# A recurrent mixer scheduled in double slots of two head pairs, its gated output kept in SBUF, and feed-forward first sums kept apart by parity

## The chip, the cores and the metric

The kernel runs on one core of one Trainium2 chip. The metric is the device time of one execution in microseconds (us), lower is better. TensorE is called PE (its weight loads PEld), VectorE DVE, ScalarE ACT, GpSimd POOL and SyncE SP in the rows.

## The reference

Two layers over 1024 tokens (2 sequences of 512) of width 512. Layer 0 is an autocorrelation mixer with a feed-forward branch; the change does not touch it. Layer 1 multiplies two branches over the same normalized input. What matters of it:

```python
# recurrent branch (8 groups of 16 heads of 64 channels, state of 128)
h = x * rsqrt(mean(x*x) + eps) * norm_w
gate, hBC, dt = split(h @ in_proj_w.T)            # 8192 | 8192 + 2*8*128 | 128
hBC = silu(causal_conv(hBC, conv_w, conv_b))      # 4 taps
hid, B, C = split(hBC)
# per head, in chunks of 128 tokens
Y_diag = (C @ B.T * exp(segsum(A*dt))) @ (hid*dt)          # within a chunk
states = carried over chunks with decay; Y_off = C @ states * exp(A_cs)
y = (Y_diag + Y_off + Dp*hid) * silu(gate)
y = y * rsqrt(mean(y*y over the group) + eps) * gnorm_w
s = x + y @ out_proj_w.T                          # the block's own input x is added
# feed-forward branch, int4 weights with one scale per 128 inputs
g = silu((silu(x @ Wg.T) * (x @ Wu.T)) @ Wd.T)
# layer output: the layer's input + s * g
```

## The kernel before, in words

Everything is float32. A large product is three passes of a 128x512 matmul on float32r halves (high by high, low by high, high by low; lines 75 to 77). Each engine runs one instruction list written out by hand; semaphores order them.

**Feed-forward.** For each of 14 channel tiles m and each sequence n, PE makes eight group products (gate and up parts, four scale groups k). ACT scales groups 0 and 1 into two first sums, `sum_a` and `sum_b` (line 994); DVE adds groups 2 and 3 (line 1137); POOL adds `sum_b` to `sum_a`; ACT takes the silu (line 999), and DVE multiplies the two `sum_a` parts into `f_inner` (line 1147). `sum_a(n, part)` is one buffer for each n and part, so ACT may start tile m only when `f_inner` of tile m-1 is made. The down products of tile m-1 are placed between the groups of tile m.

**Mixer.** A unit is one group of one sequence, 16 in all. A unit has eight head pairs k (two heads of 64 channels). While PE scans unit u it also projects unit u+1, so every slot k has, in this order: OFF (carried state times C, line 1879), DIAG (the within-chunk product, two heads side by side in column halves of 64, line 1871), ST (states, line 1835), OP (the output projection of the pair before, 12 three-pass matmuls into `s_ps_o`), T (transposes of hid, line 1827), G and H (the gate and channel projections of the next unit, 12 matmuls each into `s_ps`). Slot 2 also has the projections of C and B, slot 5 CB (line 1813), slot 6 BT, slot 0 SQ (line 1861), the transpose of the sum of squares of the unit before. `ps` has four PSUM banks that these jobs share by role; `ps_o` has the four of the output projection. A unit "-1" only projects unit 0, and the last unit only scans.

For a pair, DVE multiplies OFF by its decay (`dve_yoff`, L2173), adds the skip term to DIAG's bank (`dve_y_skip`, L2181), adds the carried part (`dve_y_carried`, L2189), and multiplies by the gate in the same PSUM bank (`dve_y_gated`, L2199). ACT rounds it to the high part (`act_y`, L2005) and squares it (`act_sq`, L2014). DVE makes the low part (`dve_y_lo`, L2140), and only that frees DIAG's bank. POOL makes the low parts of the weights (`pool_w` L2292, `pool_wo` L2314), the masked decay products (`pool_m` L2309) and the running sum of squares (`pool_sum` L2302). DVE also makes the other three taps of the convolution (L2110) and the silu into `hid`, `cT` or `bT` (L2115).

## Time and profile before

| | |
|---|---|
| median of 3 runs | 2004.83 us (2001.99 to 2005.57) |
| profiled execution: its time, its span | 2006.6 us, 2004.8 us |
| granted TensorE clock | 0.996 |
| busy: PE, PEld | 1951.4 us (97%), 1567.6 us (78%) |
| busy: DVE, ACT, POOL | 1601.0 (80%), 1484.1 (74%), 1230.7 us (61%) |
| DMA | 241.74 MB, mean 121 GB/s |

Matmuls are pipelined: the next starts before the one ahead has ended, so the busy time of PE says only that one was in flight. The distance between two starts tells what a matmul costs. In the timeline rows the first number is the start in us from the span's start, the second the duration from the first start to the last end, xN the count of instructions merged in the row, and brackets hold the idle time before it and what ended it. One float32 matmul of 128 columns is two PE instructions (a transpose is one), so OFF and ST are six and DIAG sixteen.

### The profile page before, as it was taken

How to read it: one execution, taken by the hardware profiler on the slowest of the kernel's cores; microseconds unless marked ns; L12 is line 12 of the kernel's file. 1: busy time of each engine (PE TensorE's matmuls, PEld its weight loads, DVE VectorE, ACT ScalarE, POOL GpSimd, SP SyncE). 2: the span in 40 equal slices, each digit the busy share in tenths (PEclk: the TensorE clock that was granted, in tenths of full speed). 3: DMA queues.
4: the chain of work that ended last, by engine and by line, in shares of the span. 5: the costliest groups of instructions: out<-in, count | busy, mean ns of one | idle time of the engine just before them, and what ended most of it. 6: DMA issues, size and time to landing. Idle time of an engine off the chain costs nothing.

```text
span 2004.8 us, 32751 instructions
## 1 busy us (share of the span) xinstructions
PE 1951.4 (97%) x10846; PEld 1567.6 (78%) x10846; DVE 1601.0 (80%) x2979; ACT 1484.1 (74%) x2986; POOL 1230.7 (61%) x854
## 2 busy tenths in 40 slices
PE   7998999999999999999999999999999999999998
PEld 5564666677888888888888888888888888888886
DVE  7777889857777878788878787878787878787888
ACT  5345866547787878787878787878787878787876
POOL 5644777644656666666656666565656665656666
PEclk9998999999999999999999999999999999999999
DMA  5615332544434343334333333333433333433424
GB/s 194 191 55 152 100 92 88 154 149 134 129 97 132 93 132 102 125 113 127 119 115 119 106 119 106 119 118 111 128 114 115 116 109 116 156 108 117 128 92 133
DMA packets 114472, 241.74 MB, mean 121 GB/s; under 512 B 23681, under 2 KB 24706, under 8 KB 113794
## 3 DMA queue, kind: packets, MB, share of 16 engines
q1 hardware_dynamic: 110466, 227.06, 36.2%
...
HBM read 226.75 MB, written 12.85 MB: 120 GB/s over the span
## 4 chain that ended last, share of the span: by engine, by line
PE 76%; DVE 2%; ACT 0%; issue 0%; DVEq 0%; ACTq 0%
PE s_ps L75 13%; PE s_ps L77 13%; PE s_ps L76 13%; PE s_ps L1871 6%; PE s_ps_o L75 6%; PE s_ps_o L77 6%; PE s_ps_o L76 6%; PE s_ps L1835 5%; PE s_ps L1879 4%; PE s_ps L1827 3%; PE s_ps L1813 1%; PE s_ps L1861 0%; DVE s_cv L2110 0%; PE s_ps L1819 0%; DVE s_state L2086 0%
## 5 line engine op out<-in xcount | busy, mean ns | idle before, releaser
L2292 POOL TENSOR_TENSOR w_lo<-w_raw,w_hi 128x1024 fp32r<-128x1024 f32 x142 | 340.0, 2399 | 529.7 <-ACT w_hi L1942 529.7
L75 PE MATMUL s_ps<-h_hi,w_hi 128*128 128x512 f32 x1152 | 463.0, 402 | 6.0 <-DVE s_hid L2115 4.2
L77 PE MATMUL s_ps<-h_hi,w_lo 128*128 128x512 f32 x1152 | 450.1, 391 | 0.0
L76 PE MATMUL s_ps<-h_lo,w_hi 128*128 128x512 f32 x1152 | 448.7, 390 | 0.0
L2110 DVE SCALAR_TENSOR_TENSOR s_cv<-s_ps,s_par,s_cv 128x511 f32<-128x511 f32 (+2 forms) x480 | 355.8, 744 | 15.2 <-ACT s_cv L1985 9.3
L2309 POOL TENSOR_TENSOR s_lm<-s_lm,s_cbt 128x512 f32<-128x512 f32 x256 | 326.2, 1296 | 12.2 <-ACT s_lm L1967 12.2
L1960 ACT ACTIVATE s_lm<-s_rows,s_steps 128x128 f32<-128x128 f32 x1024 | 312.5, 391 | 0.8 <-PE s_ps L1871 0.8
L1985 ACT ACTIVATE s_cv<-s_ps,s_par 128x512 f32<-128x512 f32 x160 | 124.5, 778 | 215.8 <-PE s_ps L77 215.8
L75 PEld LDWEIGHTS s_ps<-h_hi,w_hi 128*128 128x128 f32 x1152 | 216.4, 188 | 53.9 <-DVE s_hid L2115 5.6
L77 PEld LDWEIGHTS s_ps<-h_hi,w_lo 128*128 128x128 f32 x1152 | 216.2, 188 | 47.3
L76 PEld LDWEIGHTS s_ps<-h_lo,w_hi 128*128 128x128 f32 x1152 | 216.8, 188 | 41.1
L2173 DVE TENSOR_TENSOR s_yoff<-s_ps,s_scale 128x384 f32<-128x384 f32 x128 | 71.2, 556 | 188.1 <-PE s_ps L1879 187.9
L75 PE MATMUL s_ps_o<-s_wo_hi,s_y_hi 128*128 128x512 f32 x512 | 211.3, 413 | 2.0 <-DVE s_y_lo L2140 2.0
L77 PE MATMUL s_ps_o<-s_wo_hi,s_y_lo 128*128 128x512 f32 x512 | 201.1, 393 | 0.0
L76 PE MATMUL s_ps_o<-s_wo_lo,s_y_hi 128*128 128x512 f32 x512 | 199.9, 390 | 0.0
L2314 POOL TENSOR_TENSOR s_wo_lo<-s_wo_raw,s_wo_hi 128x512 fp32r<-128x512 f32 x128 | 166.2, 1299 | 0.3 <-ACT s_wo_hi L2020 0.3
L1942 ACT ACTIVATE w_hi<-w_raw 128x1024 fp32r<-128x1024 f32 x142 | 147.1, 1046 | 4.0 <-DMA w_raw<-in_w_in 3.0
L1967 ACT ACTIVATE s_lm<-s_lm 128x512 f32<-128x512 f32 x256 | 147.7, 625 | 2.8
L2302 POOL TENSOR_TENSOR s_ssq<-s_ssq,s_sq 128x512 f32<-128x512 f32 x95 | 123.0, 1295 | 41.3 <-ACT s_sq L2014 41.3
L1871 PE MATMUL s_ps<-s_lm,s_hdt 128*64 128x128 f32 x2048 | 141.0, 280 | 0.3 <-issue 0.3
L1975 ACT ACTIVATE s_scale<-s_rows 64x384 f32<-64x384 f32 x256 | 132.4, 517 | 3.1
L1991 ACT ACTIVATE s_ps<-s_cv 128x512 f32<-128x512 f32 x160 | 96.4, 602 | 45.0 <-DVE s_cv L2110 42.0
...
## 6 DMA issues: line engine op xcount, KB each, us to landing
...
s_wo_raw<-in_w_out SPq DMA_DIRECT2D x128, 256.0 KB, 3.5
...
```

Of the source, the lines that this page charges most:

```text
L75: nc.tensor.matmul(dst, l_hi, r_hi, start=start, stop=False)
L76: nc.tensor.matmul(dst, l_hi, r_lo, start=False, stop=False)
L77: return nc.tensor.matmul(dst, l_lo, r_hi, start=False, stop=stop)
L1871: mm = nc.tensor.matmul(dst[e * HP:(e + 1) * HP, c], hdt[:, k % 2, j, e * HP:(e + 1) * HP], lm[:, (2 * k + e) % 4, c], start=True, stop=True)
L1942: nc.scalar.activation(w_hi[:, slot, :], w_raw[:, slot, :], ACT.Copy).then_inc(w_hi_ready, 1)
L1960: ins = nc.scalar.activation(lm[:, h % 4, c], rows[:, h % 4, c], ACT.Relu, bias=steps[:, v.b, 2, i, h:h + 1], scale=-1.0)
L1967: nc.scalar.activation(lm[:, h % 4, :], lm[:, h % 4, :], ACT.Exp, scale=-1.0).then_inc(exp_ready, 1)
L1975: nc.scalar.activation(scale[e * HP:(e + 1) * HP, k % 2, :], rows[e * HP:(e + 1) * HP, h % 4, P:], ACT.Exp).then_inc(scale_ready, 1)
L2110: nc.vector.scalar_tensor_tensor(dst, src[:, 0:SEQ - d], par[:, v.b, 4 * j + 3 - d:4 * j + 4 - d], dst, ALU.mult, ALU.add).then_inc(conv_c ...
L2292: nc.gpsimd.tensor_tensor(w_lo[:, slot, :], w_raw[:, slot, :], w_hi[:, slot, :].bitcast(F32), ALU.subtract).then_inc(w_lo_ready, 1)
L2309: nc.gpsimd.tensor_tensor(lm[:, h % 4, :], lm[:, h % 4, :], cbt[:, v.b].rearrange("p c i -> p (c i)"), ALU.mult).then_inc(m_ready, 1)
L2314: nc.gpsimd.tensor_tensor(wo_lo[:, k % 2, :], wo_raw[:, k % 2, :], wo_hi[:, k % 2, :].bitcast(F32), ALU.subtract).then_inc(wo_lo_ready, 1)
```

## The change

It does six things.

1. **Double slots.** Units 0 to 14 run in four double slots s of pairs a = 2s and b = 2s+1. PE does OFF a, OFF b, DIAG a, DIAG b, T, G a, H a, G b, T, H b, ST, ST, OP a, OP b, with C, B, CB, BT and SQ set between, and the banks are now written in the list with each job. OP of a pair is in its own double slot, and so is the last pair's of a unit, with SQ.
2. **Gated y in SBUF.** `gated` is now `hid[:, k, :]`: `dve_y_gated` writes it over the hid tile it belongs to, and DIAG's bank is free then (`freed["DIAG"]` is `y_ready`). The silu of the next unit's tile waits for the low part of y to be made.
3. **Low part on GpSimd.** A new ACT instruction `act_scaled` multiplies the tile by the norm weight in place, and `pool_y_lo` subtracts the high part. `dve_y_lo` stays in the last unit alone.
4. **Carried part of odd pairs in `s_tg`**, the buffer of the gate's tanh, so that two pairs are in flight; ACT's gate waits for it.
5. **New first and last unit**, each with its own list. B and C are projected after pair 3 instead of pair 1 (`BC_SLOT` 4).
6. **First sums by parity.** Odd tiles m use `odd_sums`, a part of `m_group` that is not yet in use, so ACT's wait goes from tile m-1 to m-2.

```diff
+        odd_sums = group[:].rearrange("p g n -> p (g n)")[:, 0:2 * NB * SEQ].rearrange("p (s t) -> p s t", s=2 * NB)
+        def sum_a(m, n, part):
+            if m % 2:
+                return odd_sums[:, 2 * n + part, :]
...
-                if k == 0 and m:
-                    act.wait_ge(inner_ready[n], m)
+                if k == 0 and m >= 2:
+                    act.wait_ge(inner_ready[n], m - 1)
...
-BC_SLOT = 2
+PAIRS = KC // 2
+BC_SLOT = 4
+def double_jobs(s):
+    a, b = 2 * s, 2 * s + 1
+    jobs = [(C_BANK, ("OFF", 0, a)), (D_BANK, ("OFF", 0, b)), (A_BANK, ("DIAG", 0, a)), (B_BANK, ("DIAG", 0, b)),
+            (C_BANK, ("T", *divmod(a + 2, KC))), (D_BANK, ("G", 1, a)), (A_BANK, ("H", 1, tile_of(a)))]
+    if s == 3:
+        jobs += [(C_BANK, ("BT", 1, 0))]
+    jobs += [(D_BANK, ("G", 1, b)), (C_BANK, ("T", *divmod(b + 2, KC))), (B_BANK, ("H", 1, tile_of(b)))]
+    if s == 1:
+        jobs += [(A_BANK, ("H", 1, C_AT))]
+    jobs += [(C_BANK, ("ST", *divmod(a + 2, KC)))]
+    second = (D_BANK, ("ST", *divmod(b + 2, KC)))
+    if s == 1:
+        jobs += [(None, ("OP", 0, a)), (B_BANK, ("H", 1, B_AT)), second]
+    elif s == 2:
+        jobs += [second, (A_BANK, ("CB", 1, 0)), (None, ("OP", 0, a))]
+    elif s == 3:
+        jobs += [(D_BANK, ("SQ", 0, 0)), (None, ("OP", 0, a)), second]
+    else:
+        jobs += [second, (None, ("OP", 0, a))]
+    return jobs + [(None, ("OP", 0, b))]
...
-        freed = {**took, "DIAG": y_lo_ready, "H": tile_ready, "SQ": ssq_took}
+        freed = {**took, "DIAG": y_ready, "H": tile_ready, "SQ": ssq_took}
...
+        def act_scaled(act, un, k):
+            nc.scalar.activation(gated(un, k), gated(un, k), ACT.Copy,
+                                 scale=par[:, un.b, 58 + k:59 + k]).then_inc(scaled_ready, 1)
...
         def gated(un, k):
-            return tg[:] if un.last and k == KC - 1 else bank(un, ("DIAG", 0, k))
+            return hid[:, k, :]
...
+        def pool_y_lo(pool, un, k):
+            pool.wait_ge(scaled_ready, un.at(KC, k))
+            nc.gpsimd.tensor_tensor(y_lo[:, k % 2, :], gated(un, k), y_hi[:, k % 2, :].bitcast(F32),
+                                    ALU.subtract).then_inc(y_lo_ready, 1)
...
+        def pool_double(pool, un, s):
+            a, b, v = 2 * s, 2 * s + 1, un.ahead(1)
+            pool_w(pool, *load_unit(un, EARLY[s]))
+            pool_wo(pool, un, a)
+            pool_y_lo(pool, un, a)
+            if a:
+                pool_sum(pool, un, a)
+            pool_wo(pool, un, b)
+            pool_y_lo(pool, un, b)
+            pool_sum(pool, un, b)
...
+            if s == 1:
+                pool_w(pool, v, LOADS.index(("BC", 0)))
+            pool_m(pool, *pair_at(un, a + 2))
+            pool_m(pool, *pair_at(un, b + 2))
+            if load_unit(un, LATE[s]):
+                pool_w(pool, *load_unit(un, LATE[s]))
```

PE, in the middle of the mixer, from the last projection of a slot to the next three-pass product. Before (L1879 is OFF, L1871 DIAG, L1835 ST, L75 to `s_ps_o` OP):

```order
L77 MATMUL s_ps<-h_hi,w_lo 128x512
L1879 MATMUL s_ps<-s_cT,s_state 128x128 x3
L1871 MATMUL s_ps<-s_lm,s_hdt 64x128 x8
L1835 MATMUL s_ps<-s_hdd,s_b_l 128x128 x3
L75 MATMUL s_ps_o<-s_wo_hi,s_y_hi 128x512
```

The same place now (L1935 is OFF, L1927 DIAG, L1883 T):

```order
L77 MATMUL s_ps_o<-s_wo_hi,s_y_lo 128x512
L1935 MATMUL s_ps<-s_cT,s_state 128x128 x6
L1927 MATMUL s_ps<-s_lm,s_hdt 64x128 x16
L1883 MATMUL s_ps<-ident,s_hid 128x128 x4
L75 MATMUL s_ps<-h_hi,w_hi 128x512
```

Both pairs' DIAG now stand in one run, followed by a transpose instead of ST, once in two pairs where it was once in each.

DVE, the start of a slot in the middle of the mixer. Before, the y chain (L2181, L2189, L2199) has convolution and state steps between its parts:

```order
L2173 TENSOR_TENSOR s_yoff<-s_ps,s_scale 128x384
L2110 SCALAR_TENSOR_TENSOR s_cv<-s_ps,s_par,s_cv 128x511
L2110 SCALAR_TENSOR_TENSOR s_cv<-s_ps,s_par,s_cv 128x510
L2081 COPY s_state<-s_ps 128x128
L2181 SCALAR_TENSOR_TENSOR s_ps<-s_hid,s_skip,s_ps 128x512
L2086 SCALAR_TENSOR_TENSOR s_state<-s_state,s_cdecay,s_ps 128x64 x2
L2110 SCALAR_TENSOR_TENSOR s_cv<-s_ps,s_par,s_cv 128x509
L2086 SCALAR_TENSOR_TENSOR s_state<-s_state,s_cdecay,s_ps 128x64 x2
L2189 TENSOR_TENSOR s_ps<-s_ps,s_yoff 128x384
L2199 TENSOR_TENSOR s_ps<-s_ps,s_gate 128x512
```

The same place now (L2288, L2296 and L2304 are the y chain):

```order
L2280 TENSOR_TENSOR s_yoff<-s_ps,s_scale 128x384
L2280 TENSOR_TENSOR s_tg<-s_ps,s_scale 128x384
L2288 SCALAR_TENSOR_TENSOR s_ps<-s_hid,s_skip,s_ps 128x512
L2296 TENSOR_TENSOR s_ps<-s_ps,s_yoff 128x384
L2304 TENSOR_TENSOR s_hid<-s_ps,s_gate 128x512
L2288 SCALAR_TENSOR_TENSOR s_ps<-s_hid,s_skip,s_ps 128x512
L2296 TENSOR_TENSOR s_ps<-s_ps,s_tg 128x384
L2304 TENSOR_TENSOR s_hid<-s_ps,s_gate 128x512
L2230 SCALAR_TENSOR_TENSOR s_gate<-s_tg,s_ps 128x512
```

The y chains of two pairs stand back to back at the head of the double slot, and the convolution and state steps come behind them.

POOL, the double slot in which the weights of B and C are split (L2518 is `pool_wo`, L2513 `pool_y_lo`, L2501 `pool_sum`, L2508 `pool_m`, L2491 `pool_w`), now:

```order
L2518 TENSOR_TENSOR s_wo_lo<-s_wo_raw,s_wo_hi 128x512
L2513 TENSOR_TENSOR s_y_lo<-s_hid,s_y_hi 128x512
L2501 TENSOR_TENSOR s_ssq<-s_ssq,s_sq 128x512
L2518 TENSOR_TENSOR s_wo_lo<-s_wo_raw,s_wo_hi 128x512
L2513 TENSOR_TENSOR s_y_lo<-s_hid,s_y_hi 128x512
L2501 TENSOR_TENSOR s_ssq<-s_ssq,s_sq 128x512
L2491 TENSOR_TENSOR w_lo<-w_raw,w_hi 128x1024
L2508 TENSOR_TENSOR s_lm<-s_lm,s_cbt 128x512 x4
```

The weights' low part stands behind two y low parts that POOL did not make before.

## Rows read from the trace of the kernel before

**Rows 1.** Windows: start:end, length, busy PE, PEld, DVE, ACT, POOL, PEclk, DMA, GB/s.

```profile
221.69:371.31 149.62, 141.40 (x571) 101.70 (x570) 132.02 (x170) 101.98 (x170) 107.88 (x77) 1.00 0.31 92
...
424.93:481.23 56.30, 53.01 (x242) 43.29 (x242) 35.50 (x56) 33.71 (x59) 19.78 (x10) 1.00 0.45 135
481.23:1941.79 1460.56, 1459.20 (x8731) 1216.01 (x8730) 1174.32 (x2293) 1163.59 (x2396) 915.41 (x606) 1.00 0.38 117
1941.79:2004.80 63.01, 52.25 (x371) 43.65 (x369) 52.80 (x111) 45.41 (x103) 38.72 (x31) 0.95 0.39 126
```

**Rows 2.** Timeline of PE, one slot in the middle of the mixer.

```profile
1006.71 0.83 PE L1879 MATMUL s_ps<-s_cT,s_state 128*128 128x128 f32 x6
1007.47 1.09 PE L1871 MATMUL s_ps<-s_lm,s_hdt 128*64 128x128 f32 x16
1008.49 0.94 PE L1835 MATMUL s_ps<-s_hdd,s_b_l 128*128 128x128 f32 x6
1009.18 0.48 PE L75 MATMUL s_ps_o<-s_wo_hi,s_y_hi 128*128 128x512 f32 x1
...
1012.02 0.60 PE L1827 MATMUL s_ps<-ident,s_hid 128*128 128x128 f32 x4
1012.38 0.48 PE L75 MATMUL s_ps<-h_hi,w_hi 128*128 128x512 f32 x1
...
1017.92 0.83 PE L1879 MATMUL s_ps<-s_cT,s_state 128*128 128x128 f32 x6
```

**Rows 3.** Timeline of PE in three windows under 0.2 us: OFF, then DIAG.

```profile
1007.04 0.50 PE L1879 MATMUL s_ps<-s_cT,s_state 128*128 128x128 f32 x3
...
1007.74 0.49 PE L1871 MATMUL s_ps<-s_lm,s_hdt 128*64 128x128 f32 x5
...
1008.18 0.38 PE L1871 MATMUL s_ps<-s_lm,s_hdt 128*64 128x128 f32 x3
```

**Rows 4.** Timeline of PE where DIAG is followed by SQ, and ST by OP.

```profile
1943.57 0.66 PE L1861 MATMUL s_ps<-ident,s_ssq 128*128 128x128 f32 x4
1944.06 0.83 PE L1835 MATMUL s_ps<-s_hdd,s_b_l 128*128 128x128 f32 x6
1944.65 0.47 PE L75 MATMUL s_ps_o<-s_wo_hi,s_y_hi 128*128 128x512 f32 x1
```

**Rows 5.** Timeline of PE, the CB products of two units in turn.

```profile
1811.94 1.06 PE L1813 MATMUL s_ps<-s_cT,s_bT 128*128 128x128 f32 x8
...
1909.44 0.83 PE L1813 MATMUL s_ps<-s_cT,s_bT 128*128 128x128 f32 x6
```

**Rows 6.** Timelines of DVE, ACT and POOL in the slot of rows 2.

```profile
1009.69 0.75 DVE L2181 SCALAR_TENSOR_TENSOR s_ps<-s_hid,s_skip,s_ps 128x512 f32<-128x512 f32 x1
...
1011.76 0.56 DVE L2189 TENSOR_TENSOR s_ps<-s_ps,s_yoff 128x384 f32<-128x384 f32 x1
1012.36 0.70 DVE L2199 TENSOR_TENSOR s_ps<-s_ps,s_gate 128x512 f32<-128x512 f32 x1
...
1014.17 0.67 ACT L2005 ACTIVATE s_y_hi<-s_ps,s_par 128x512 fp32r<-128x512 f32 x1
...
1008.71 2.40 POOL L2292 TENSOR_TENSOR w_lo<-w_raw,w_hi 128x1024 fp32r<-128x1024 f32 x1 [7.08 <-ACT w_hi L1942]
...
1013.55 1.33 POOL L2314 TENSOR_TENSOR s_wo_lo<-s_wo_raw,s_wo_hi 128x512 fp32r<-128x512 f32 x1
```

**Rows 7.** Timelines of ACT, DVE and POOL in the feed-forward, around tile 10.

```profile
334.48 0.69 ACT L994 ACTIVATE m_wdt<-m_ps,f_gu_s 128x512 f32<-128x512 f32 x1 [3.30 <-DVE f_inner L1147]
...
336.30 0.69 DVE L1147 TENSOR_TENSOR f_inner<-f_sum_a 128x512 f32<-128x512 f32 x1 [0.23 <-ACT f_sum_a L999]
...
343.92 1.65 DVE L1147 TENSOR_TENSOR f_inner<-m_wdt,f_sum_a 128x512 f32<-128x512 f32 x1
...
343.73 2.97 POOL L1427 TENSOR_TENSOR f_sum_a<-f_sum_a,g_stage 128x512 f32<-128x512 f32 x2
```

**Rows 8.** Waits of PE: us in total, times, longest; 424.9 to 500, then 1941 to 2005.

```profile
PE s_ps L75 <- DVE s_hid L2115: 4.2, 3, 2.1
...
PE s_ps L1827 <- DVE s_hid L2115: 2.1, 1, 2.1
```

698 lines of the change are left out of this document (426 added, 272 removed).

## The prediction, made before the changed kernel was run

> **What bounds the kernel now.** I read the windows by stage first, then the timeline of PE inside one slot, then the other engines in that slot. In the windows the reader is to see that units 0 to 14 take 1460.56 us, that PE is in flight for 1459.20 of them, and that DVE and ACT are at about 80% and POOL at 63% [rows 1]. So nothing done on DVE, ACT or POOL can shorten this stage; only what PE itself issues, or how tightly, can. The feed-forward is different: PE idles 8.2 us of 149.6, while DVE is busy for 132.0. The first unit has 3.3 us of idle PE, the rest from 1941.79 on 10.8 us [rows 1], part of it the tail after the last matmul.
>
> A PE that is always busy can still be slow. Between two starts OFF costs 0.11 us an instruction [rows 2, 3], so its six should take 0.66; DIAG starts 0.76 after it. DIAG's sixteen come as eight couples of 0.11 [rows 3], 0.88 in all, but ST starts 1.02 later. ST then takes 0.69 to the next product [rows 2], where it takes 0.59 if it stands behind SQ and not behind DIAG [rows 4]. So going into half-width matmuls and out again costs 0.10 + 0.14 + 0.10 = 0.34 us, in each pair.
>
> **The change, part by part.**
>
> *Fewer switches on PE.* Matmuls, loads and passes stay the same; the order changes. Before, two pairs pay 0.68. Now one run of two DIAG pays once: 0.10 at the entrance, 0.14 in the run, and then a transpose, not ST. For that exit the nearest row is SQ behind DIAG: 0.49 for four transposes against 4 x 0.11 = 0.44, so 0.05 [rows 4]. Together 0.29, a gain of 0.39 a double slot. With 4 double slots in 15 units that is 60 x 0.39 = 23.4 us. Lower bound: if the second DIAG paid like the first, the gain is 0. Upper bound: all 0.34 of one pair and all 0.10 of the exit, 0.44, is 26 us. I take 23.4, since inside a DIAG the couples follow at 0.11 without any such cost. The changes between three-pass products and small float32 groups also become a little fewer, but T and its successor show 0.36 for four [rows 2], no dearer than 0.11 each, so I cost them at nothing.
> The Trainium skill, TensorEngine Tiling (Array Packing), Key Properties, says that changing the tiling mode drains TensorE. By it alone both exits would cost the same, the gain would be 0.34 a double slot and 20.4 us in all; the row of SQ puts it 3 us higher.
>
> *Small waits inside the slots.* Two CB products in turn are 97.50 us apart, one unit [rows 5]. Eight slots of 11.21 (1006.71 to 1017.92) are 89.7; the projections of C and B are 2 x 2.77 (half of 1012.38 to 1017.92) = 5.5; CB, BT and SQ are 8, 3 and 4 instructions of 0.11, 1.65 [rows 2, 3]. That is 96.9, so 0.6 a unit is waiting hidden in the busy time: 9.4 us over 15 units. The new order removes those places and makes others. I followed one double slot from the start of OFF a. OFF takes 1.3 and DIAG a is written at 2.6. DVE's chain for a is 0.75 + 0.56 + 0.70, done at 4.7. Then ACT: y_hi (0.67), the square and the new `act_scaled`, for which the trace has no row; between nothing and two of y_hi's 0.67 I take 0.6, done at 6.4. POOL then has five instructions of 1.3 (y low part, sum and `wo` low part for the two pairs) and, in double slot 1, the 2.40 us split of the B and C weights: 15.3 [rows 6]. PE wants these weights after OFF, DIAG, T, four projections and T: 3.3 + 0.5 + 4 x 2.77 + 0.4 = 15.3. So they meet, with no slack. Two more places meet within 0.2: BT behind DVE's turning of pair a, and H of B behind the silu of tile b. Everywhere else I find 0.6 us or more. Bounds: nothing, and 1.5 us a unit (22 us), if each of the three is half a microsecond late. I take 0.5 a unit, 7.5 us. In unit 14 two POOL products of 1.3 stand ahead of that split, 2.5 us once.
> Mixer: -23.4 - 9.4 + 7.5 + 2.5 = -22.8 us.
>
> *Work moved.* `dve_y_lo` leaves DVE 120 times and comes to POOL: 915.4 + 120 x 1.3 = 1071 us of about 1438, 75%. ACT gets 120 `act_scaled`: 1163.6 + 72 = 1236 us, 86% [rows 1, 6]. Both stay under PE's time, which hides them; without that cover `act_scaled` would cost 72 us. The consumer, OP a, comes 16.7 us into the double slot and y's low part is made at 7.8; OP b has 7 us as well. ACT's new wait for the carried part of b (done at about 6) queues tanh of G a behind it; tanh, then DVE's gate product, free the bank of G b by 8.2, and PE comes there at 9.4. SP's list is reordered too: rows of decay for the next double slot are asked for when the scales are made, late in the double slot, and used behind a weight split in the next one; they land in time or ACT, which then waits for y_ready anyway, hides it.
>
> *Feed-forward by parity.* ACT waits 3.30 us at each tile for `f_inner` of the tile before (sequence 1), which DVE makes only behind the sums of the present tile, and PE stands behind ACT [rows 7]. This wait goes. PE's idle of 8.2 us over 13 tiles is mainly its echo. Late next is DVE: 132.0 busy of 149.6 [rows 1], so the stage can't go under some 135. I take 8.5 us, the idle time plus a little of what is stretched by late weight loads. Bounds: 3 (DVE's order holds it) and 13.
>
> *First unit.* PE waits three times there for the silu that frees a bank, 4.2 us [rows 8]. The new list puts ST 0 and ST 1 ahead of the last H and G, and T further back. At its end DIAG of pair 0 needs the silu of tile 7, whose tap, three taps, tanh and silu take about as long as G and the two OFF; I keep 1.2 us of waiting. Gain 3, bounds 0 and 5.
>
> *Last unit.* T waits 2.1 us for a silu [rows 8]; tile 7 is now ready sooner. But OP 0 now comes early and must wait for DVE to have taken the output sums of the unit before. And `dve_y_lo` there reads two SBUF operands: the product of two SBUF operands took 0.69 alone and 1.65 beside POOL's sums [rows 7]. Over 7 of them that is up to 6.7 us, of which DVE's 10.2 idle us in this stage [rows 1] hide a part. I take 2 lost there and 2 won at the start: 0, bounds -3 and +5.
> The Trainium skill, SBUF, Who interferes with whom, speaks against this one: a DVE instruction with two SBUF inputs and a GpSimd one that reads SBUF exclude each other. The two rows agree, 0.69 against 1.65. In the double slots no DVE instruction has two SBUF tensors, so the low parts moved to POOL don't touch it.
>
> **Sum.** -22.8 - 8.5 - 3 + 0 = -34.3 us. The durations are of the profiled execution, 2006.6 us (span 2004.8), which would be 1972; against the median of 2004.83 it is 1970.5. I say 1971.
>
> **The rivals.**
> 1. *As forecast*, 1971, own range 1960 to 1983. Chance 0.62.
> 2. *All new waits vanish and the feed-forward gains its 13*: 2004.8 - 32.8 - 13 - 5 = 1954; 1950 to 1960. For it: the double slots have slack of 0.6 and more nearly everywhere. Chance 0.08.
> 3. *POOL becomes late.* It is the engine that got the new work, in front of the weights of B and C. If these are 1.3 us late, one POOL instruction more than I count, and the other two places take 0.3 together, a unit loses 1.6: 24 us instead of 7.5, and the time is 1971 + 16.5 = 1987; 1983 to 2000. Against: POOL has a quarter of its time free. Chance 0.14.
> 4. *The second DIAG pays like the first.* Each brings new weights at half width. Then 23.4 us are not won: 1994. Against: the couples at 0.11 [rows 3]. Chance 0.06.
> 5. *Slower: the loop between double slots.* Gate, silu and y chain of DVE and ACT form a ring: the silu of tile b closes a double slot, the next y chains stand behind it back to back, then tanh, gate and only then G b. The slack is 9.4 - 8.2 = 1.2 us. Beyond it PE loses one for one. ACT has 86% of its time taken; each place where it waits for DVE in the fixed order counts. If the ring is late by 1.8 us, PE loses 0.6 in each of 60, 36 us, and the change decides against itself; at 2.2 us late it is 60, and the time 2031. Before, y of a pair could start without the silu of a whole double slot ahead of it. Against: by my count DVE ends a double slot no more than 1.2 us into the next one, and y of a can't start before 2.6. Chance 0.10.
>
> **How the numbers follow.** The time is that of rival 1. For 8 in 10 I take 1958 to 1991: 0.62, three quarters of the 0.14, and a little of 2 and 4. A measurement of this kernel can tell 0.2%, 4 us, from no change. Faster: 0.62 + 0.08 + nearly all of 0.14 and 0.06, lowered to 0.87; the same 0.04; slower 0.09.
>
> **What would show it.** In the changed trace: DIAG of two pairs about 1.9 us from first start to T, T to G 0.49; CB products 95.3 to 96 us apart; no PE wait over 0.5 us in units 0 to 13; feed-forward tiles 10.9 us apart on the mean where 149.6 / 13 = 11.5 stood [rows 1], and ACT's wait of 3.3 us gone. Wrong would be a wait of PE for `w_lo` or for a `s_hid` or `s_gate` product in each double slot, or a second gap of 0.2 between the two DIAG.

## The result, and the profile after

The changed kernel takes 1988.86 us (median of 4 executions, 1986.19 to 1992.09) where the kernel before, on the same chip, takes 2004.56. The ratio is 0.9924, 95% interval 0.9906 to 0.9942. A second series on another chip gave 1986.83 us (5 executions) and 0.9912, 0.9899 to 0.9926 (e9 below). So it is faster by 16 to 18 us; 34 were forecast. Two series of the same kernel differ by 2 us, so a difference of that size between kernels of different series says nothing, and small effects are read from stages of the traces. That has a limit too: the last unit takes 61.3 to 61.6 us in some traces and 64.4 or more in others with the same instructions in it (see e2), so there a difference of 3 us between two traces shows little.

The busy times of the profile, to set beside the table of before:

```profile
PE 1930.7 (97%) x10846; PEld 1565.7 (79%) x10846; DVE 1562.3 (79%) x2859; ACT 1554.9 (78%) x3106; POOL 1387.1 (70%) x974
```

Windows of the changed kernel by stage, columns as in [rows 1]: feed-forward tiles 1 to 13, unit -1, units 0 to 14, last unit; then unit 14 alone, and the feed-forward tiles 6 and 9:

```profile
217.81:364.15 146.34, 140.49 (x568) 102.35 (x567) 129.25 (x168) 104.62 (x169) 109.90 (x77) 1.00 0.31 94
...
418.89:473.46 54.57, 53.49 (x248) 43.72 (x249) 36.67 (x62) 33.27 (x57) 21.32 (x11) 1.00 0.39 124
473.46:1924.59 1451.13, 1442.67 (x8747) 1215.64 (x8746) 1134.70 (x2175) 1234.85 (x2523) 1064.79 (x725) 1.00 0.39 118
1821.45:1924.59 103.14, 97.82 (x585) 82.13 (x584) 79.78 (x147) 82.25 (x168) 76.09 (x52) 0.98 0.34 102
1924.59:1986.08 61.49, 47.61 (x349) 39.40 (x347) 54.42 (x104) 42.48 (x100) 40.92 (x30) 0.97 0.41 133
275.47:287.86 12.39, 11.04 (x45) 7.95 (x45) 11.66 (x18) 7.44 (x13) 8.86 (x6) 1.00 0.30 86
311.16:322.05 10.89, 10.89 (x46) 7.95 (x45) 8.96 (x13) 7.46 (x13) 8.84 (x6) 1.00 0.34 99
```

The span is 1986.1 us, 18.7 less than before. Tile 1 starts 3.9 us earlier (217.81, was 221.69), in code that the change doesn't touch, and in e2, which has the feed-forward of before, it starts at 216.27; so that is no gain of the change. Units 0 to 14 are 9.4 us shorter, although OP of pair 7 and SQ (twelve products of 0.23 and 0.4 us, 3.2 in all) now belong to their own unit: 12.6 us like for like, forecast 22.8. The first unit is 1.7 shorter and has ST 1 besides (0.6): 2.3 to 2.4, forecast 3. The last lost this work (3.2 + 0.6 = 3.8 us) and is only 1.5 shorter: 2.3 dearer like for like, forecast 0. The feed-forward tiles take 146.3 where the same stretch, up to the start of the last group, was 149.1: 2.8 gained, forecast 8.5. The down products behind them are 0.6 longer.

Timeline of PE, a double slot in the middle (to be held against [rows 2]), and the CB products of two units in turn:

```profile
1362.72 1.50 PE L1935 MATMUL s_ps<-s_cT,s_state 128*128 128x128 f32 x12
1364.15 1.97 PE L1927 MATMUL s_ps<-s_lm,s_hdt 128*64 128x128 f32 x32
1366.05 0.66 PE L1883 MATMUL s_ps<-ident,s_hid 128*128 128x128 f32 x4
1366.46 0.48 PE L75 MATMUL s_ps<-h_hi,w_hi 128*128 128x512 f32 x1
...
1407.33 1.06 PE L1867 MATMUL s_ps<-s_cT,s_bT 128*128 128x128 f32 x8
...
1503.51 1.06 PE L1867 MATMUL s_ps<-s_cT,s_bT 128*128 128x128 f32 x8
```

From start to start: OFF 1.43, the run of two DIAG 1.90, the transposes 0.41. At 0.11 an instruction (0.055 for each of DIAG's thirty-two) that is 1.32, 1.76 and about 0.36, so 0.11 in, 0.14 in the run, 0.05 out. That is the forecast of the switches (0.10, 0.14, 0.05) within 0.01. The unit is 96.18 us (97.50 in [rows 5]), where 95.8 was forecast.

From OFF to OFF the four double slots of a steady unit take 22.19, 27.94, 23.02 and 23.03 us, unit after unit. Small waits can be seen at three places, 0.6 us in all. The start of the first double slot (a row of the chain that ended last), where DIAG takes 0.18 us longer than the 1.90 above (in the third double slot 0.1):

```profile
1342.03 2.08 PE s_ps L1927 x32
```

And the projection of C in the second double slot: first POOL, then the weight load of PE (L2513 is y's low part, L2501 the sum of squares, L2491 the weights' low part):

```profile
1373.12 1.30 POOL L2513 TENSOR_TENSOR s_y_lo<-s_hid,s_y_hi 128x512 fp32r<-128x512 f32 x1
1374.39 1.28 POOL L2501 TENSOR_TENSOR s_ssq<-s_ssq,s_sq 128x512 f32<-128x512 f32 x1
1375.64 2.40 POOL L2491 TENSOR_TENSOR w_lo<-w_raw,w_hi 128x1024 fp32r<-128x1024 f32 x1
...
1378.15 0.19 PEld L75 LDWEIGHTS s_ps<-h_hi,w_hi 128*128 128x128 f32 x1 [0.51 <-DVE s_hid L2225]
```

Two things are due here. The hid tile that the row names, whose silu frees the bank, was made at 1377.87, and the weights at 1378.04, 15.3 us after OFF; PE loads at 1378.15. So the weights end the wait, but by 0.17 us only. PE could have started at 1377.91, 15.2 us after OFF, and starts at 1378.18: a wait of 0.3 us a unit. The prediction had 15.3 for both sides.

Unit 14 takes 103.14, 7 us more than a steady unit, and only 2.5 were forecast. PE's waits in it, and a DVE row from the end of its third double slot, two totals of the output behind the last silu; the carried part of the next double slot, which frees bank C, starts only at 1903.22:

```profile
PE s_ps L75 <- POOL w_lo L2491: 2.5, 1, 2.5
PE s_ps L1883 <- DVE s_yoff L2280: 1.8, 1, 1.8
PE s_ps L1875 <- DVE s_hdt L2205: 0.9, 1, 0.9
```

```profile
1898.64 4.66 DVE L1752 TENSOR_TENSOR xs<-xs,s_end_x 128x512 f32<-128x512 f32 x2
```

The first wait is the forecast one. The two others come from the totals: two additions of two SBUF tensors take 4.66 us and stand ahead of the carried parts. They make the fourth double slot 26.01 us instead of 23.03. The second takes 31.94 instead of 27.94, which is more than the wait of 2.5. The rest is TensorE's clock: right behind that wait the granted clock is at its half level, 1.2 GHz, and the products follow at 0.43 us instead of 0.23.

```profile
1862.30:1865.70 3.40, 3.40 (x10) 2.62 (x9) 0.79 (x2) 0.48 (x1) 3.40 (x4) 0.50 0.82 286
```

In e3, e6, e8 and e13 the same wait is not followed by such a stretch, and the double slot takes 30.4 us. So the 7 us are 2.4 for the weights, 1.6 for the clock and 3.0 for the totals. What decides whether the clock falls behind this wait is not shown.

In the feed-forward ACT's wait of 3.30 us is gone, as forecast, and the fast tiles are bound by PE alone (tile 9: PE 10.89 of 10.89). But tile 6 has 11.66 us of DVE work in 12.39. PE's waits between 217 and 365 us, before and then now:

```profile
PE m_ps L941 <- DVE m_wdt L1137: 2.8, 2, 1.4
PE m_ps L941 <- ACT m_wdt L994: 2.7, 5, 0.7
PE m_ps L941 <- ACT f_sum_a L994: 1.7, 2, 0.9
PE m_ps L941 <- ACT g_stage L994: 0.7, 1, 0.7
```

```profile
PE m_ps L945 <- DVE m_group L1142: 2.6, 3, 1.4
PE m_ps L945 <- ACT f_sum_a L998: 1.7, 2, 0.9
PE m_ps L945 <- DVE m_wdt L1142: 1.5, 2, 1.3
```

Behind ACT PE lost 5.1 us and loses 1.7 now; behind DVE it lost 2.8 and loses 4.1.

### The profile page after: what moved, and what is told of

It reads as the page before. It is cut to its first block, busy times and chain, and to the rows that moved or that the text cites. A ratio compares the mean times of both kernels' runs of the same rounds, so it can differ in the third digit from the quotient of the medians.

```text
span 1986.1 us, 33129 instructions
## 1 busy us (share of the span) xinstructions
PE 1930.7 (97%) x10846; PEld 1565.7 (79%) x10846; DVE 1562.3 (79%) x2859; ACT 1554.9 (78%) x3106; POOL 1387.1 (70%) x974
## 4 chain that ended last, share of the span: by engine, by line
PE 72%; DVE 3%; ACT 2%; issue 1%; POOL 1%; DVEq 0%; ACTq 0%; POOLq 0%
PE s_ps L75 13%; PE s_ps L76 13%; PE s_ps L77 12%; PE s_ps L1927 6%; PE s_ps_o L75 5%; PE s_ps_o L77 5%; PE s_ps_o L76 5%; PE s_ps L1891 4%; PE s_ps L1935 4%; PE s_ps L1883 3%; PE s_ps L1867 1%; DVE s_cv L2217 1%; ACT s_scale L2023 0%; PE s_ps L1875 0%; ACT s_lm L2008 0%
## 5 line engine op out<-in xcount | busy, mean ns | idle before, releaser
L2491 POOL TENSOR_TENSOR w_lo<-w_raw,w_hi 128x1024 fp32r<-128x1024 f32 x142 | 337.8, 2388 | 223.9 <-ACT w_hi L1991 223.9
L75 PE MATMUL s_ps<-h_hi,w_hi 128*128 128x512 f32 x1152 | 463.5, 402 | 6.8 <-POOL w_lo L2491 2.5
L2508 POOL TENSOR_TENSOR s_lm<-s_lm,s_cbt 128x512 f32<-128x512 f32 x256 | 326.1, 1296 | 123.4 <-ACT s_lm L2015 123.0
L2008 ACT ACTIVATE s_lm<-s_rows,s_steps 128x128 f32<-128x128 f32 x1024 | 318.4, 389 | 34.3 <-PE s_ps L1927 34.3
L75 PEld LDWEIGHTS s_ps<-h_hi,w_hi 128*128 128x128 f32 x1152 | 216.8, 188 | 54.6 <-DVE s_hid L2225 8.9
L77 PEld LDWEIGHTS s_ps<-h_hi,w_lo 128*128 128x128 f32 x1152 | 216.7, 188 | 46.6
L75 PE MATMUL s_ps_o<-s_wo_hi,s_y_hi 128*128 128x512 f32 x512 | 209.2, 409 | 2.2 <-DVE s_y_lo L2309 2.2
L2513 POOL TENSOR_TENSOR s_y_lo<-s_hid,s_y_hi 128x512 fp32r<-128x512 f32 x120 | 155.4, 1295 | 74.4 <-ACT s_hid L2067 74.4
L2039 ACT ACTIVATE s_ps<-s_cv 128x512 f32<-128x512 f32 x160 | 95.8, 599 | 104.1 <-DVE s_cv L2217 103.9
L2518 POOL TENSOR_TENSOR s_wo_lo<-s_wo_raw,s_wo_hi 128x512 fp32r<-128x512 f32 x128 | 166.3, 1299 | 4.0 <-ACT s_wo_hi L2074 4.0
L2053 ACT ACTIVATE s_y_hi<-s_hid,s_par 128x512 fp32r<-128x512 f32 x128 | 92.0, 719 | 67.0 <-DVE s_hid L2304 66.9
L2230 DVE SCALAR_TENSOR_TENSOR s_gate<-s_tg,s_ps 128x512 f32<-128x512 f32 x128 | 87.4, 683 | 68.1 <-ACT s_tg L2046 68.0
L2225 DVE SCALAR_TENSOR_TENSOR s_hid<-s_ps,s_cv 128x512 f32<-128x512 f32 x128 | 87.9, 686 | 65.7 <-ACT s_ps L2039 65.6
```

The source lines that it names most:

```text
L75: nc.tensor.matmul(dst, l_hi, r_hi, start=start, stop=False)
L77: return nc.tensor.matmul(dst, l_lo, r_hi, start=False, stop=stop)
L2008: ins = nc.scalar.activation(lm[:, h % 4, c], rows[:, h % 4, c], ACT.Relu, bias=steps[:, v.b, 2, i, h:h + 1], scale=-1.0)
L2491: nc.gpsimd.tensor_tensor(w_lo[:, slot, :], w_raw[:, slot, :], w_hi[:, slot, :].bitcast(F32), ALU.subtract).then_inc(w_lo_ready, 1)
L2508: nc.gpsimd.tensor_tensor(lm[:, h % 4, :], lm[:, h % 4, :], cbt[:, v.b].rearrange("p c i -> p (c i)"), ALU.mult).then_inc(m_ready, 1)
L2513: nc.gpsimd.tensor_tensor(y_lo[:, k % 2, :], gated(un, k), y_hi[:, k % 2, :].bitcast(F32), ALU.subtract).then_inc(y_lo_ready, 1)
```

## The experiments

Each is an edit of the changed kernel where nothing else is said. The ratios are to the kernel before on the same chip.

**e1: parity alone.** The kernel before with part 6 only.

> The kernel before with the first sums by parity alone. Theory A, from the trace after: ACT's wait goes, but POOL's sums and DVE's chain behind them set the pace of a tile, so tiles 1 to 13 shrink by 2 to 4 us and the time is 2001 to 2003. Theory B, the forecast: PE's idle time of 8.2 us goes, 1996.

Measured 2001.27 us (11 executions), ratio 0.9985, 0.9977 to 0.9994. Its tiles 1 to 13, by the same view as above:

```profile
218.93:365.23 146.30, 140.49 (x568) 102.36 (x567) 129.18 (x169) 104.77 (x170) 109.47 (x77) 1.00 0.31 94
```

So part 6 is worth 3 us (the interval says 1 to 5), and the tiles take 146.3 us with it in either kernel.

**e2: mixer alone.** The changed kernel with the feed-forward of before.

> The changed kernel with the feed-forward as before. Theory A: the mixer brings some 13 to 15 us of the change, 1990 to 1992. Theory B, that the double slots bring little and the rest came from the feed-forward and from chance: 1996 or more. The slots of a steady unit should be as in the changed kernel, 96.16 us a unit.

Measured 1991.58 us, 0.9944, 0.9930 to 0.9958: 11 to 13 us. With e1's 3 the two parts add up to 14 to 16, the result within its spread. Its steady units are those of the changed kernel (96.16 us), but its last unit, where no instruction differs, takes 64.6 us and not 61.5. PE waits 2.2 us there for y's low part in the changed kernel, and here:

```profile
PE s_ps_o L75 <- DVE s_y_lo L2304: 7.8, 7, 1.4
```

The low parts take 1.07 us on the mean in the one trace and 1.45 in the other. So the same list of instructions has a short and a long course in the last unit; e5, e9 and e10 have the short one, e3, e7, e11 and e12 a long one. What decides between them is not shown.

**e3: DIAG apart.** T stands between the two DIAG, so the half-width run is cut in two.

```diff
-    jobs = [(C_BANK, ("OFF", 0, a)), (D_BANK, ("OFF", 0, b)), (A_BANK, ("DIAG", 0, a)), (B_BANK, ("DIAG", 0, b)),
-            (C_BANK, ("T", *divmod(a + 2, KC))), (D_BANK, ("G", 1, a)), (A_BANK, ("H", 1, tile_of(a)))]
+    jobs = [(C_BANK, ("OFF", 0, a)), (D_BANK, ("OFF", 0, b)), (A_BANK, ("DIAG", 0, a)),
+            (C_BANK, ("T", *divmod(a + 2, KC))), (B_BANK, ("DIAG", 0, b)), (D_BANK, ("G", 1, a)), (A_BANK, ("H", 1, tile_of(a)))]
```

> The changed kernel with T set between DIAG a and DIAG b, so that PE enters and leaves the half-width form twice in a double slot. Theory A, the price of the switches: about 0.3 us in each of 60 double slots, 17 to 20 us slower than the changed kernel, 2006 to 2009, and DIAG a to the end of DIAG b 0.3 us longer. Rival: the gain came from something else in the order of the slots, and the time stays within 4 us of the changed kernel.

Measured 2010.67 us, 1.0031, 1.0021 to 1.0042: slower than the kernel before and some 21 us slower than the changed kernel. So nearly the whole gain hangs on the joined run; how much of it is the price of switching shows inside a double slot. Timeline of PE in a double slot where nothing waits:

```profile
1085.06 1.09 PE L1927 MATMUL s_ps<-s_lm,s_hdt 128*64 128x128 f32 x16
1086.08 0.66 PE L1883 MATMUL s_ps<-ident,s_hid 128*128 128x128 f32 x4
1086.66 1.09 PE L1927 MATMUL s_ps<-s_lm,s_hdt 128*64 128x128 f32 x16
1087.69 0.50 PE L75 MATMUL s_ps<-h_hi,w_hi 128*128 128x512 f32 x1
```

1.02 + 0.58 + 1.03 = 2.63 from DIAG to G, where 1.90 + 0.41 = 2.31 stood: a second run costs 0.32 us. In 60 double slots that would be 19 us. In the first and third T also waits for DVE to take bank C, in the first 0.41 us:

```profile
1356.88 0.66 PE L1883 MATMUL s_ps<-ident,s_hid 128*128 128x128 f32 x4 [0.41 <-DVE s_yoff L2280]
```

Its four double slots take 22.86, 27.94, 23.66 and 23.25 us, which is 0.67, 0, 0.64 and 0.22 more than in the changed kernel. In the second the added 0.32 is not to be seen: PE comes later to the projection of C, and waits less for it. So of the 1.5 us that a unit lost some 0.85 are switches (13 us in all) and 0.7 waits of T. An edit that parts the two DIAG without moving T would have kept the two apart; none was run.

**e4: totals and products late.** In unit 14 POOL's products stand behind the last weight split of their double slot, and DVE's totals behind the first turning of double slots 2 and 3.

```diff
-            if un.u == UNITS - NB and 1 <= s <= 2:
-                pool_product(pool, 1, 2 * s - 2)
-                pool_product(pool, 1, 2 * s - 1)
             if s == 1:
                 pool_w(pool, v, LOADS.index(("BC", 0)))
...
             if load_unit(un, LATE[s]):
                 pool_w(pool, *load_unit(un, LATE[s]))
+            if un.u == UNITS - NB and 1 <= s <= 2:
+                pool_product(pool, 1, 2 * s - 2)
+                pool_product(pool, 1, 2 * s - 1)
...
                 dve_out(dve, un.ahead(-1))
+            if un.u == UNITS - NB and s >= 2:
+                dve_total(dve, 1, s - 2)
...
-            if un.u == UNITS - NB and s == 2:
-                dve_total(dve, 1, 0)
-                dve_total(dve, 1, 1)
```

> The changed kernel with unit 14's four POOL products behind the late weight split of their double slot, and its two DVE totals in double slots 2 and 3 behind the turning of pair a. Theory A: unit 14's 7 us over the others came from the products ahead of the split of the B and C weights (PE waits 2.5 us for w_lo and 2.9 more) and from the totals ahead of the next carried part; double slots of 31.94 and 26.01 us fall to about 28.5 and 24, 4 to 6 us less, 1983 to 1985. Rival: the products only move their delay to the next weight split, and no more than 2 us come back.

Measured 1984.7 us, 0.9903, 0.9888 to 0.9917. Windows of unit 14 and of the last unit:

```profile
1819.74:1915.96 96.22, 96.10 (x585) 80.96 (x583) 78.22 (x147) 81.75 (x168) 76.32 (x52) 1.00 0.37 108
1915.96:1982.60 66.64, 50.32 (x349) 41.02 (x347) 56.97 (x104) 43.10 (x100) 41.64 (x30) 0.92 0.38 125
```

Unit 14 is a steady unit now, 6.9 us shorter, so its 7 us came from the order of these instructions; the low stretch of the clock behind the wait is gone with the wait. But the last unit is 5.2 us longer than in the changed kernel. Some 3 of these are in e2's last unit too, which has nothing of this edit. For the rest the clock is enough: from 1923.7 to 1930.5 us it was granted at its half level, with PE in flight for 5.35 us; at 0.43 us a product instead of 0.23 that costs some 2.5 us, an estimate.

**e5: down scales late.** DVE scales the down weights behind the sums of sequence 1 and not ahead of `f_inner`.

```diff
-                dve_scale_down(dve, m + 1)
+                if m == 0:
+                    dve_scale_down(dve, m + 1)
...
                     dve_groups(dve, m, 1)
+                    if m:
+                        dve_scale_down(dve, m + 1)
...
+            dve_scale_down(dve, KI)
```

> The changed kernel with DVE's product of down weights and scales behind the sums of sequence 1 in each feed-forward tile, not ahead of f_inner of sequence 0. Theory A: that product reads two SBUF operands and holds up POOL's two sums, which take 3.5 us beside it where two take 2.6; f_inner, the next sums and PE wait for them. Moved, the tiles of 10.9 us fall to 10.3 to 10.6, 3 to 6 us less than the changed kernel, 1983 to 1986. Rival: DVE's total work sets the tile, so the order doesn't matter and the time stays within 2 us.

Measured 1992.27 us, 0.9938, 0.9924 to 0.9951: nothing gained, and tiles 1 to 13 took 147.3 us (146.3 in the changed kernel). This other order of the same DVE work doesn't shorten the stage.

**e6: last low parts on POOL.** The last unit makes y's low part as the double slots do, on ACT and POOL.

```diff
-            if un.last:
-                ins.then_inc(scaled_ready, 1)
...
                 act_sq(act, un, k)
+                act_scaled(act, un, k)
...
-                dve_y_lo(dve, un, k)
...
                 pool_wo(pool, un, k)
+                pool_y_lo(pool, un, k)
```

> The changed kernel with the last unit's low part of y also on ACT and POOL. Theory A: DVE's instruction with two SBUF operands took 1.6 us beside POOL where 0.7 stood, and the last six slots of 6.2 to 7.1 us fall to about 6.0: 3 to 5 us less, 1984 to 1986. Rival: POOL, with 1.3 us more in each short slot of 5.9 us, becomes the late one there, and the slots grow to 6.4 or more: no gain, 1989 or slower.

Measured 1992.46 us, 0.9939, 0.9925 to 0.9952: no gain, as the rival had it. The last unit takes 66.4 us, 4.9 more than in the changed kernel, and PE waits 6.6 us for the low part in six places, where it waits 2.2 us in three there. The long course of e2, with 7.8 us of such waiting, still takes 1.8 us less; the trace of e6 has 3.4 us at the half clock besides.

**e7: weights of B and C ahead of a sum.** In double slot 1 POOL splits them ahead of the sum of pair b, and ACT's tap of tile a stands ahead of the second four decay rows (here `act_diff`).

```diff
-            act_diff(act, ua, 2 * a_on + 1)
+            if s != 1:
+                act_diff(act, ua, 2 * a_on + 1)
             act_tap(act, v, tile_of(a), h_a)
+            if s == 1:
+                act_diff(act, ua, 2 * a_on + 1)
...
             pool_y_lo(pool, un, b)
-            pool_sum(pool, un, b)
+            if s != 1:
+                pool_sum(pool, un, b)
...
             if s == 1:
                 pool_w(pool, v, LOADS.index(("BC", 0)))
+                pool_sum(pool, un, b)
```

> The changed kernel with POOL's split of the B and C weights ahead of the sum of squares of pair b, and ACT's tap of tile a ahead of the second decay difference, in double slot 1. Theory A, of the waits: the projection of C waits 0.3 us for the silu of tile a and for this split together, so the double slot falls from 27.94 to about 27.6 and the kernel by 4 to 5 us, 1984 to 1985. Rival: another wait (H of B, or the next G) takes it back and the unit stays at 96.2 us.

Measured 1985.23 us, 0.9903, 0.9888 to 0.9918. That looks like a gain, but a steady unit has none: double slot 1 takes 27.94 us as before. POOL now waits for ACT's high part of these weights (its y low part ended at 1086.73), and a second wait comes up at the projection of B:

```profile
1087.50 2.41 POOL L2494 TENSOR_TENSOR w_lo<-w_raw,w_hi 128x1024 fp32r<-128x1024 f32 x1 [0.77 <-ACT w_hi L1991]
...
1090.21 0.19 PEld L75 LDWEIGHTS s_ps<-h_hi,w_hi 128*128 128x128 f32 x1 [0.23 <-DVE s_hid L2228]
1096.70 0.19 PEld L75 LDWEIGHTS s_ps<-h_hi,w_hi 128*128 128x128 f32 x1 [0.47 <-DVE s_hid L2228]
```

The idle of the load at 1090.21 fell to 0.23 us (0.51 in the row above); the one at 1096.70, for the silu that frees B's bank, is new. In unit 14 alone the edit helps: double slot 1 takes 29.1 us there (31.9, or 30.4 at full clock). The difference of the medians, 3.6 us to the first series and 1.6 to the second, is not clear of the spread between series.

**e8: root in the next unit.** ACT takes the root of the sum of squares at the start of the next unit and not at the end of double slot 3, where its two table loads stand ahead of the last silu.

```diff
             act_w(act, *load_unit(un, EARLY[s]))
+            if s == 0 and not un.first:
+                act_rms(act, un.ahead(-1))
...
-            if s == 3:
-                act_rms(act, un)
...
         def act_end(act, un):
+            act_rms(act, un.ahead(-1))
```

> The changed kernel with the square root and its two table loads (2.9 us of ACT) in the first double slot of the next unit, not ahead of the last tanh of a unit. Theory A: there they delay the silu of tile b and DVE's next carried part, DIAG b waits 0.2 us in the first double slot of each unit, and the last unit starts 2 us late. Moved, the first double slot falls from 22.19 to about 22.05, and the last unit starts without its wait: 3 to 4 us less, 1985. Rival: the loads delay y of pair a and the gate in the first double slot instead, which grows: same or slower.

Measured 1997.0 us, 0.9963, 0.9949 to 0.9976, slower than the changed kernel. The first double slot went from 22.19 to 22.61, 6 us over the units: DIAG there lost its 0.18, and tanh and gate behind the root became late. The last unit took 66.0 us. Between 480 and 1860 us the trace has 14 waits of PE for the gate, 4.4 us in all, where that of the changed kernel has no wait of PE.

**e9: the changed kernel again**, beside e10 to e12.

> The changed kernel itself, once more, beside the three kernels that are built on it, since its own median of four executions (1988.86 us) and those of the kernels made from it come from different chips. If the small differences read so far are real, it gives 1988 to 1990 us and about 0.9925 of the kernel before, with double slots of 22.19, 27.94, 23.02 and 23.03 us and feed-forward tiles as already seen. If the chips differ by more than that, it gives something else, and the differences of 3 to 4 us between kernels of different chips mean nothing.

Measured 1986.83 us, 0.9912, 0.9899 to 0.9926. Its stages are those of the first trace within 0.4 us from tile 1 to the end, but for 0.9 in the down products.

**e10: step sums spread.** `dve_sums` is left with the product, and `dve_scans` has its four scans.

```diff
-                if m in (6, 7):
-                    dve_sums(link, m - 6)
+                if m in (6, 8):
+                    dve_sums(link, m // 2 - 3)
+                if m in (7, 9):
+                    dve_scans(m // 2 - 3)
```

> The changed kernel, with one edit in the feed-forward: the step product and the four scans of DVE, which both stand in tile 6 for sequence 0 and in tile 7 for sequence 1, now stand in tiles 6 (product), 7 (scans), 8 (product) and 9 (scans). Theory A: a tile takes what its fullest engine needs, and in tiles 6 and 7 that is DVE with 11.66 us of work, while PE needs 10.9 us; the mean over the stage hid this. Then tiles 6 and 7 fall from 12.39 us each to about 11, tiles 8 and 9 stay at 10.9, and the kernel gains 2 to 3 us. Rival: the tiles are long because POOL's sums and DVE's products with two SBUF inputs exclude each other; the work that is moved does not change that, the long pair of tiles stays or moves, and the kernel gains nothing.

Measured 1989.11 us, 0.9921, 0.9908 to 0.9935: no gain. Windows of tiles 6, 7, 8 and 9 (12.39, 12.39, 10.91 and 10.89 us in the changed kernel):

```profile
275.81:286.93 11.12, 11.04 (x44) 7.95 (x45) 10.39 (x14) 7.43 (x13) 8.85 (x6) 1.00 0.33 96
286.93:298.86 11.93, 11.00 (x44) 7.94 (x45) 11.23 (x17) 7.43 (x13) 8.86 (x6) 1.00 0.30 88
298.86:310.00 11.14, 11.02 (x44) 7.95 (x45) 10.41 (x14) 7.43 (x13) 8.86 (x6) 1.00 0.16 47
310.00:321.87 11.87, 11.02 (x44) 7.95 (x45) 11.87 (x17) 7.33 (x13) 8.19 (x6) 1.00 0.05 21
```

The work moved as meant, and the tile lengths moved with it: 46.1 us in the four where 46.6 stood. In tile 9 DVE has 1.4 us of scans more, but 2.9 us more busy time (11.87, was 8.96): two of its products of two SBUF tensors, 0.68 us each in the changed kernel, take 1.80 and 1.39, since they now run beside POOL's instructions. So a tile is long where DVE is full, as Theory A said, but the work that is moved grows where it lands, and the rival's "no gain" holds.

**e11: two waits of double slot 1.** The edit of e7, and ACT's tap of tile b one row group earlier.

```diff
-            act_diff(act, ub, 2 * b_on + 1)
+            if s != 1:
+                act_diff(act, ub, 2 * b_on + 1)
             act_tap(act, v, tile_of(b), h_b)
+            if s == 1:
+                act_diff(act, ub, 2 * b_on + 1)
```

> The edit of e7 (the weights of B and C split ahead of the sum of squares of pair b in double slot 1), and one more: ACT's first tap of tile b stands ahead of the second four decay rows of its pair in double slot 1. In e7 PE's wait at the projection of C fell from 0.33 to 0.1 us, but a wait of 0.2 us came up at the projection of B, for the silu of tile b, and the double slot stayed at 27.94 us. Theory A: two chains end side by side there, and both have to be shortened: double slot 1 falls to 27.6 to 27.7 us, and 15 units gain 3 to 5 us over the changed kernel beside it. Rival: a third chain ends there too (ACT, which has 86% of its time taken, or the rows of decay that POOL multiplies), the double slot stays at 27.9 us, and there is no gain.

Measured 1985.92 us, 0.9901, 0.9886 to 0.9916. Double slot 1 takes 27.79 us, for the first time under 27.9, but above the 27.6 to 27.7 of Theory A. So both chains were real, and others remain. 0.15 in 15 units is 2 us; the median is 0.9 under that of e9, which is within the spread of either.

**e12: e4, e10 and e11 together.**

> The edits of e4 (POOL's products and DVE's totals of unit 14 placed later), e10 and e11 in one kernel. If they act in different places, their gains add: 4 us of e4, 2 to 3 of e10 and 3 to 5 of e11 make 1977 to 1980 us where the changed kernel beside it takes 1989. If the waits are taken over by one another, as in e7, it stays at 1983 to 1986 us, what e4 alone gave.

Measured 1983.52 us, 0.9898, 0.9883 to 0.9913; 3.3 us under e9 and inside the rival's 1983 to 1986. Unit 14 takes 96.0 us, but the last unit 66.7. Of the groups of DVE's instructions in its last unit, this is y's low part:

```profile
L2320 DVE SCALAR_TENSOR_TENSOR s_y_lo<-s_hid,s_par,s_y_hi 128x512 fp32r<-128x512 f32 x8 | 11.2, 1402 | 0.8 <-ACT s_y_hi L2058 0.8
```

1402 ns on the mean (0.75 to 1.79 us). This left the last unit as the open question.

**e13: last unit's gated y in PSUM**, part 2 undone there for pairs 0 to 6.

```diff
-                    pe.wait_ge(freed[kind], u * TURNS[kind] + i + 1)
+                    sem_at = y_lo_ready if kind == "DIAG" and owner.last else freed[kind]
+                    pe.wait_ge(sem_at, u * TURNS[kind] + i + 1)
...
         def gated(un, k):
-            return hid[:, k, :]
+            return bank(un, ("DIAG", 0, k)) if un.last and k < KC - 1 else hid[:, k, :]
...
         def dve_y_lo(dve, un, k):
-            dve.wait_ge(y_hi_ready, un.at(KC, k))
+            dve.wait_ge(scaled_ready, un.at(KC, k))
```

> The changed kernel, with part 2 of the change undone in the last unit alone: the gated product of pairs 0 to 6 stays in DIAG's PSUM bank there, as it did before, so that DVE's low part reads one SBUF tensor and not two, and the bank is free only after the low part (which waits for ACT's square). Theory A: DVE's low parts of 1.0 to 1.7 us in the last unit are the lock between DVE with two SBUF inputs and POOL; from PSUM they take 0.75 us, and the last unit falls from 61.5 to 59 us, a gain of 2 to 3 us. Rival: the last unit is set by POOL's sums and products in a row, or by the later freeing of the bank; the low parts get shorter, but another wait takes their place, and the last unit stays within 1 us of 61.5.

Measured 1985.37 us, 0.9909, 0.9893 to 0.9926, which can't be told from the changed kernel. The low part in the last unit, first in the changed kernel, then here:

```profile
L2309 DVE SCALAR_TENSOR_TENSOR s_y_lo<-s_hid,s_par,s_y_hi 128x512 fp32r<-128x512 f32 x8 | 8.5, 1068 | 0.8 <-ACT s_y_hi L2053 0.8
```

```profile
L2310 DVE SCALAR_TENSOR_TENSOR s_y_lo<-s_ps,s_par,s_y_hi 128x512 fp32r<-128x512 f32 x7 | 5.2, 743 | 0.3 <-ACT s_sq L2063 0.3
```

Every one of the seven takes 0.74 to 0.75 us now, POOL beside it or not, where those from SBUF took up to 1.64. The window of its last unit is 1.6 us under the 61.49 of the changed kernel, between the 59 of Theory A and the rival, and 4.7 under the long course of e2:

```profile
1921.33:1981.20 59.87, 46.72 (x349) 39.06 (x347) 51.51 (x104) 41.93 (x100) 38.35 (x30) 0.97 0.41 136
```

PE waits as long for the low part as in the changed kernel (2.3 and 2.2 us). What is gone is this wait, of DIAG for the gated product that freed its bank:

```profile
PE s_ps L1927 <- DVE s_hid L2304: 1.8, 2, 0.9
```

**e14: e12 and e13 together.**

> The edits of e12 and that of e13. In e4 and e12 the second slot of the last unit took 12 us and PE waited there for DVE's low parts; so the edit should be worth more here. Theory A: last unit 3 to 5 us shorter than in e12, and 1979 to 1981 us. Rival: the two totals that e4 moved behind, and not the low part, hold the second slot, and the time stays within 1 us of e12, at 1983.

Measured 1979.34 us (4 executions, 1975.95 to 1982.93), 0.9883, 0.9863 to 0.9903: the lowest median of all, 24 us under the kernel before. Its interval and that of e12 overlap, so the step from e12 is read from the stages. Unit 14 and the last unit:

```profile
1818.55:1914.59 96.04, 96.04 (x584) 80.93 (x583) 78.55 (x147) 81.84 (x168) 76.31 (x52) 1.00 0.35 108
1914.59:1974.60 60.01, 46.74 (x349) 39.11 (x347) 51.14 (x104) 42.43 (x100) 38.43 (x30) 0.96 0.40 138
```

Here the 7 us of e4 stay: the last unit is 60.0 us where e4 had 66.6 and e12 66.7. The second slot of the last unit, 11.9 us in e4 and 12.1 in e12, is 8.6, and PE's wait for the low part fell from 7.0 us to 2.3. Theory A holds, and the unit gained more than its 3 to 5 us. Not all of this is the low part itself: e12's trace has 6.8 us at the half clock early in its last unit, and here there is none before the last 5 us.

## Why the prediction was right in its core and wrong in its size

The sign was right, and so was the mechanism of the largest term, the switches of PE. The gain was half of what was forecast. By stages the shortfall is 19 us: 10.2 in units 0 to 14, 5.7 in the feed-forward tiles, 2.3 in the last unit, and 1.2 in the first unit and the down products. The step that cost most is that of the feed-forward, PE's idle time read as an echo of ACT's wait; then come the small waits and unit 14, whose terms were too small. Step by step:

- **Switches, -23.4.** Right in mechanism and price. The rows give 0.30 us a double slot where 0.29 was forecast, and in e3 a second run costs 0.32. The rival that the second DIAG pays like the first is ruled out.
- **Small waits, -9.4 and +7.5.** The net of 1.9 gained became 3.6 lost: a unit went to 96.18, not 95.8, which is 0.37 in each of 14 to 15 units, some 5 us. A part of the switches went there too: e3 shows that double slot 1 takes 27.94 us with or without the second switch, since the weights of C come when they come. The steps followed engine by engine were good: the weights were due at 15.3 us and came at 15.3. Some luck was in that: POOL starts on y at 6.6 us, not 6.4 (`act_scaled` takes 0.71 us where I had taken 0.6), and its five instructions take 6.3, not 6.5. The size failed on reading "they meet with no slack" as a chance of a wait instead of a wait; and the wait of DIAG in the first and third double slots I hadn't found. The waits that can be seen are 0.6 a unit, of 0.84 that the count of 95.3 leaves; the rest I haven't placed.
- **Unit 14, +2.5.** Measured 7. The term priced POOL's two products in front of the weights, and those cost the 2.4 forecast. It left out DVE's two totals in the same unit, 4.66 us of two-SBUF additions in front of the chain that frees PE's bank: 3.0 us. ("In the double slots no DVE instruction has two SBUF tensors" is wrong for this unit, and right for the others.) And it left out the clock, which cost 1.6 behind the wait. e4 shows that with another order of these instructions all of it goes.
- **Feed-forward, -8.5.** Measured 2.8 (e1: 3 us alone). This is the largest failure. The step that failed was "PE's idle of 8.2 us is mainly its echo", and the floor of 135 came from the stage's mean for DVE. ACT's wait did go, but PE lost only 5.1 us behind ACT before and still loses 1.7, and behind DVE itself it now loses 4.1 (2.6 + 1.5) where it lost 2.8. Tiles 4 to 7 hold DVE's extra work for the step sizes, and they are 12.0 to 12.7 us long (12.0 to 12.4 before), tiles 8 to 12 are 10.6 to 10.9. The mean of 129 us in 146 hid tiles that are full and tiles with 1.9 us to spare. e10 moved a part of that work and e5 the scaling of the down weights, and neither gained. In e10 DVE's products were seen to stretch where they met POOL; for e5 that was not looked at.
- **First unit, -3.** By its window 2.3 to 2.4, but the term was of waits, and one of them falls behind the window. The DIAG of pair 0 waits for the silu of tile 7, as the prediction said; the start of the mixer then has 0.61, 0.47 and 1.63 us of waiting, 2.7 in all, where 1.2 was kept. Before it was 4.2, so 1.5 were gained and not 3. ("No PE wait over 0.5 us in units 0 to 13" fails here, and only here.) The last of these waits makes the first double slot of unit 0 23.7 us, where later ones take 22.19; the kernel before had 1.1 of its 4.2 us inside unit 0 too.

```profile
476.59 1.97 PE L1927 MATMUL s_ps<-s_lm,s_hdt 128*64 128x128 f32 x32 [1.63 <-DVE s_hid L2225]
```

- **Last unit, 0.** Measured +2.3 in a trace with the short course and, with e2's 64.6 us, +5.4 in the long one. T's wait of 2.1 us went, as forecast. The low part from two SBUF tensors was the stated loss: in the long course (e12) it takes 1402 ns on the mean and PE waits 7.0 us for it, where from PSUM (e14) it waits 2.3. In the short course PE's wait for it is no longer than before (2.2 and 2.0), and e13 wins 1.6 on the window. The rule of the Trainium skill that the prediction weighed there, SBUF — State Buffer, Who interferes with whom (a DVE instruction with two SBUF inputs and a GpSimd one that reads SBUF exclude each other), agrees with these rows: 743 ns from PSUM, 1068 and 1402 on the mean from SBUF, and 751 for the last of them, beside which POOL does nothing.
- **POOL and the ring between double slots.** Neither rival came. In units 0 to 14 POOL is busy for 1065 us (1071 forecast) and ACT for 1235 (1236 forecast). The ring was priced at 0.6 us of waiting in each double slot; a steady unit shows 0.6 us in all its four.

The sum of what was measured is -12.6 - 2.8 - 2.4 + 2.3 + 0.6 = -14.9 by stages; with the 3.9 us before tile 1 it is the 18.7 by which the span is shorter. The medians say 16 to 18.
